# Reciprocals of softmax row sums: from a VectorE instruction to a GpSimd power of -1

## The reference

```python
q = (x @ Wq) ...; k = (x @ Wk) ...; v = (x @ Wv) ...     # 16 query heads, 4 key/value heads, 64 wide, rotary
attn = einsum('bhqd,bhkd->bhqk', q, k) / sqrt(64) + slopes * rel
attn = softmax(attn, axis=-1)                            # rows of 256 keys, for 16 heads x 256 queries
x = layernorm(x + (attn @ v) @ Wo)
x = layernorm(x + windowed_cross_attention(x, context))
x = layernorm(x + quantised_gated_ffn(x))
```

## Time and profile before

| | |
|---|---|
| median of 3 runs | 2327.14 us |
| the profiled execution, its own time | 2328.01 us |
| its span, first to last instruction | 2326.2 us |
| instructions | 54958 |
| mean granted TensorE clock | 0.985 |
| TensorE busy (matmul) | 2229.3 us, 96% |
| VectorE busy | 1976.2 us, 85% |
| ScalarE busy | 1568.7 us, 67% |
| GpSimd busy | 1220.2 us, 52% |

### The profile page before, as it was taken

One profiled execution on the slowest core, in us unless ns is written; L12 is line 12 of the kernel. 1 busy time (PEld: TensorE's weight loads), 2 busy tenths in 40 slices (PEclk: granted clock), 3 DMA queues, 4 the chain that ended last, 5 costly groups with the idle time before them and its releaser, 6 DMA issues.

```text
span 2326.2 us, 54958 instructions
## 1 busy us (share of the span) xinstructions
PE 2229.3 (96%) x18218; PEld 1644.8 (71%) x18218; DVE 1976.2 (85%) x8167; ACT 1568.7 (67%) x4449; POOL 1220.2 (52%) x1390
## 2 busy tenths in 40 slices
PE   5899999999999999999999999999999999999974
PEld 4666677777777777777777777777777777777752
DVE  5778888888888888888888888888888888888865
ACT  2477666777766777767677766677776667776741
POOL 2445555555555555565555555555556555555531
PEclk8899999999999999999999999999999999999997
DMA  5000110110011111011011001111101111100100
GB/s 169 27 11 24 28 36 26 35 36 23 23 36 35 27 36 30 18 34 36 27 35 35 22 24 35 34 28 35 31 15 35 35 27 35 36 22 23 36 10 14
DMA packets 84662, 74.69 MB, mean 32 GB/s; under 512 B 18336, under 2 KB 79136, under 8 KB 84384
## 3 DMA queue, kind: packets, MB, share of 16 engines
q1 hardware_dynamic: 84384, 71.19, 11.3%
HBM read 45.98 MB, written 8.39 MB: 23 GB/s over the span
## 4 chain that ended last, share of the span: by engine, by line
PE 83%; DVE 9%; ACT 3%; POOL 2%; issue 2%; SPq 1%; DMA 1%; DVEq 0%; POOLq 0%; ACTq 0%
PE bank L444 20%; PE bank L456 11%; PE bank L539 9%; PE bank L558 9%; PE bank L462 9%; PE bank L569 8%; PE bank L610 3%; PE bank L636 3%; PE bank L617 3%; PE bank L688 2%; PE bank L449 2%; PE bank L665 2%; PE bank L675 2%; POOL qx_tok L1200 2%; DVE q_sin L858 1%
## 5 line engine op out<-in xcount | busy, mean ns | idle before, releaser
L1177 POOL TENSOR_TENSOR prob<-prob,precs 128x512 f32<-128x512 f32 x512 | 542.9, 1076 | 381.9 <-DVE precs L821 381.8
L1092 ACT ACTIVATE prob<-prob,nmax 128x256 f32<-128x256 f32 x1024 | 508.2, 498 | 260.1 <-DVE nmax L814 260.1
L814 DVE CUSTOM_DVE_ANT_0 prob<-bank,alibi 128x256 f32<-128x256 f32 x1024 | 372.8, 420 | 63.7 <-PE bank L539 58.9
L1099 ACT COPY pT<-bank 128x512 f32<-128x512 f32 x512 | 298.7, 583 | 143.9 <-PE bank L444 143.9
L1116 ACT ACTIVATE px<-px,nmx 128x128 f32<-128x128 f32 x1024 | 314.0, 392 | 70.0 <-DVE nmx L919 70.0
L444 PE MATMUL bank<-ident,prob 128*128 128x128 f32 x2048 | 316.6, 277 | 10.1 <-ACT pT L1099 8.4
L444 PEld LDWEIGHTS bank<-ident,prob 128*128 128x128 f32 x2048 | 237.7, 141 | 79.1 <-issue 43.7
L539 PE MATMUL bank<-kk,qq 64*128 64x256 f32 x2048 | 291.9, 404 | 0.7 <-DVE nmax L814 0.7
L919 DVE CUSTOM_DVE_ANT_0 px<-bank,mask 128x128 f32<-128x128 f32 x1024 | 225.7, 284 | 44.2 <-PE bank L617 32.6
L558 PE MATMUL bank<-pT,v_sb 128*64 128x256 f32 x2048 | 249.3, 385 | 0.0
L539 PEld LDWEIGHTS bank<-kk,qq 64*128 64x128 f32 x2048 | 177.5, 187 | 55.1 <-issue 34.7
(11 more groups left out here) (194 smaller groups left out, 5004.1 us busy)
## 6 DMA issues: line engine op xcount, KB each, us to landing
xT<-in_xT SPq DMA_DIRECT2D x32, 256.0 KB, 4.1
kx_tok<-in_ctx SPq DMA_DIRECT2D x32, 256.0 KB, 3.7
cT<-in_ctxT SPq DMA_DIRECT2D x32, 256.0 KB, 2.8
xtok<-in_x SPq DMA_DIRECT2D x32, 256.0 KB, 3.0
kx<-k_sin SPq DMA_DIRECT2D x256, 32.0 KB, 2.0
vs<-vx SPq DMA_DIRECT2D x64, 128.0 KB, 2.5
out_y<-y SPq DMA_DIRECT2D x32, 256.0 KB, 2.2
cellk<-in_cell SPq DMA_DIRECT2D x32, 64.0 KB, 3.7
```

The source lines that it names most:

```text
L814: v.tensor_tensor_reduce(out=prob[:, (2 * p + q) % SLOTS, c, :], in0=psum[SCORES[c]][:, q * L:(q + 1) * L], in1=alibi[:, p % 2, c, :], sca ...
L1092: nc.scalar.activation(prob[:, (2 * p + q) % SLOTS, c, :], prob[:, (2 * p + q) % SLOTS, c, :], ACT.Exp, bias=nmax[:, i:i + 1], scale=-1.0, ...
L1099: nc.scalar.copy(pT[:, p % 2, :, :, q * P:(q + 1) * P].rearrange("p c k n -> p (c k) n"), bank[:].rearrange("p (c n) -> p c n", c=4)).then ...
L1177: g.tensor_tensor(prob[:, n % SLOTS, :, :], prob[:, n % SLOTS, :, :], precs[:, 2 * n:2 * n + 2].unsqueeze(2).to_broadcast([P, 2, L]), ALU. ...
```

## The change

VectorE's part of `R n` goes. GpSimd's part now waits for the exponentials itself, adds one to a spare semaphore, makes `precs` with a tensor_tensor of `psums` and a 128x2 tile of -1.0 under the operation `pow`, and waits for the end of that before it multiplies. The tile of -1.0 is set once at the start, which is one more memset on GpSimd. Nothing is moved in the three lists.

```diff
+        minus_one = sb("minus_one", [P, 2])
...
-        POOL_CONSTS = 8
+        POOL_CONSTS = 9
...
@@ VectorE
-                    elif kind == "R":
-                        n, = args
-                        dve.wait_ge(*at("p_exp", b, 2 * n + 1))
-                        v.reciprocal(precs[:, 2 * n:2 * n + 2], psums[:, 2 * n:2 * n + 2]).then_inc(sem["p_recip"], 1)
@@ GpSimd
                     elif kind == "R":
                         n, = args
+                        pool.wait_ge(*at("p_exp", b, 2 * n + 1))
+                        pool.sem_inc(waits_passed, 1)
+                        g.tensor_tensor(precs[:, 2 * n:2 * n + 2], psums[:, 2 * n:2 * n + 2], minus_one[:], ALU.pow).then_inc(sem["p_recip"], 1)
                         pool.wait_ge(*at("p_recip", b, n))
                         g.tensor_tensor(prob[:, n % SLOTS, :, :], prob[:, n % SLOTS, :, :],
                                         precs[:, 2 * n:2 * n + 2].unsqueeze(2).to_broadcast([P, 2, L]), ALU.mult)\
                             .then_inc(sem["p_norm"], 1)
...
+            g.memset(minus_one[:], -1.0).then_inc(pool_consts, 1)
             g.memset(ones[:], 1.0).then_inc(pool_consts, 1)
-            pool.wait_ge(pool_consts, 5)
+            pool.wait_ge(pool_consts, 6)
```

## The result

The changed kernel takes 2340.40 us (median of 4, 2338.92 to 2341.13) against 2327.05 us of the kernel before (median of 4, 2326.09 to 2327.27): the ratio is 1.0057, with a 95% interval of 1.0040 to 1.0075. It is **slower by some 13 us**, where 2.6 were forecast, and 1.4 us outside the range. The profiled execution took 2338.92 us, 10.91 more than the one of before (2328.01).

What follows compares the result with a forecast made beforehand. TensorE was taken as the bound, with rounds adding 0. First and last batches summed to +2.6 us, giving 2330.6 against the profiled 2328.01, or 2329.7 us for the median; range 2325 to 2339.

Steps and rivals of the forecast that it cites:

- T 9: In each BODY round, behind R 9 after `X1`: its margin falls from 1.1 to 0.3 us, the tightest of 16.
- A: Slower: R 9 behind `X1` grows by over 1.1 us, T 9 waits in every round; 2342 us, chance 0.1.
- B: Slower: at each round's second HC, R 14's multiply starts before waiting VectorE; +27 us, 2354 us, chance 0.06.
- C: Faster: VectorE's relief removes TensorE's waits at XQ and NO, half those in first batches; -9 us, 2318 us, chance 0.06.
- R starts when the exponentials are there: In every R step: gives back up to 8 us of queueing wherever GpSimd was idle.
- a: First batches, `qtok` at 73.40: R 10 behind the next `qtok` ends 0.8 us later, delaying T 10; +0.8 us.
- b: First batches, three R steps at 181.45 push `y_rstd` to 188.9, needed by VectorE at 188.07; +0.9 us.
- c: First batches, two longer R steps ahead of `YS` delay the norm; the shift of QN comes late; +0.4 us.
- d: First batches, four R steps at 278.44: the second ends 1.6 us later, T 7 starts at 281.32; +0.8 us.
- f: Last batches, two R steps at 2188.53 end at 2192.2, `QX` had started at 2191.06, TensorE waiting; +1.1 us.
- Term e: Last batches, two R steps kept QN's shift until 2178.64; it now starts when VectorE's scale is ready; -0.7 us.
- GpSimd against VectorE: Port conflict at a BODY round's HC steps: a power holds VectorE's second HC 0.3 us, covered by idle time; 0.

Runs made afterwards that it cites:

- the repeat: The changed kernel itself measured once more, on the chip of three later runs, against the kernel before: 2339.06 us, ratio 1.0052.
- the run with the cheap operation: Changed kernel with the power replaced by a multiplication by the same -1 tile on GpSimd, same waits: 2325.98 us against 2327.00, ratio 0.9998.

## Why the prediction was wrong

**The bound and the rounds: right.** The work of a round did not get longer: the lag stays at 9.3 to 10.4 us over all 27, and the three waits of the stage are equal to 0.1 us. T 9 kept 0.3 us of margin, as forecast, although the first power behind X1 was itself held by VectorE's rounding of the first HC:

```profile
1051.98 1.16 POOL L1175 TENSOR_TENSOR precs<-psums,minus_one 128x2 f32<-128x2 f32 x1
1053.22 1.04 POOL L1177 TENSOR_TENSOR prob<-prob,precs 128x512 f32<-128x512 f32 x1
...
1054.58 0.59 PEld L445 LDWEIGHTS bank<-ident,prob 128*128 128x128 f32 x4
```

The first multiply ends at 1054.26. Rivals A and B did not happen, nor C: without its reciprocals in the rounds VectorE bought nothing (ratio 0.9992). What was only half seen is why the rounds hold. "R starts when the exponentials are there" was entered as a help wherever GpSimd was idle, and the cost as hidden in idle time; the run with both a power and a reciprocal shows that without this help each round would cost 0.68 us at XQ and NO. Both places were named in the rivals, but neither rival had this cause.

**The price: right.** 697 ns in the median (758 in the mean, with the powers that were held) and 78 ns of gap, against 720 and 80.

**The terms a to f: mostly right.** Found (forecast): a 0.6 to 1.1 (0.8), b 0.7 to 0.9 (0.9), c 0.8 (0.4), d 0.4 to 0.7 (0.8), f 1.0 (1.1). Term e (-0.7) is not to be found in the changed kernel's trace. Nor does any run show the 0.7 us counted for VectorE's relief in the first and last batches: the one stretch in which TensorE caught up is there without that relief too. Not counted were 0.9 us at V, where GpSimd's multiply of R 2 ran beside products of VectorE, and 0.6 at 227. With four steps back on VectorE the measured loss is 4.0 us by the medians and 4.9 by the ratio (1.0021 of 2327), nearer to the forecast's 2.6 and within its own range of 2325 to 2335.

**The step that failed** is the part "GpSimd against VectorE". It went through the port's conflict in a round of BODY only, at the two HC steps, and the list for the first batches went by queueing alone. But the first batches hold VectorE's one-time steps (the split of Wo, prep 7, prep 8), with operations of 128x2048 that take 1.2 to 2.3 us each, two or three in a row. This term was put at nothing. Two T steps became late by 2.7 and 2.0 us (3.3 less 0.65, and 4.6 less 2.6, in the lag), and the work behind both, at the low clock, cost 1.8 and 2.1: 8.6 us (7.8 in the repeat). One step back on VectorE gives 5.05 us; VectorE waiting for that same step gives 3.64 us with all powers in place; four steps back give 8. For the first of the two places the cause is shown by experiment. At the second the hold is seen in the traces, and its price is not parted from that of three longer steps.

The working was wrong in a second place, with no price here. It let a power that runs across the start of the second HC hold VectorE for 0.3 us. The opposite is seen, in all 27 rounds:

```profile
1070.75 0.99 POOL L1175 TENSOR_TENSOR precs<-psums,minus_one 128x2 f32<-128x2 f32 x1 [0.74 <-ACT prob L1089]
...
1071.02 0.68 DVE L1014 TENSOR_SCALAR hq<-hh 128x1024 bf16<-128x1024 f32 x1
```

The power began 0.27 us before the rounding, and the rounding took its plain 0.68 us; it was the power that took 0.29 us more.

**The Trainium skill**, "SBUF — State Buffer", section "SBUF: two separate sides", says that a GpSimd operation and a VectorE operation in a two-port mode or with two SBUF inputs exclude each other: whichever starts first has the shared pair for the whole instruction, and the other fully blocks. For the multiply the runs agree: begun 0.25 us ahead of the cast, it kept its 1.04 us, and the cast took 1.87 and not 1.22. For the power they don't: begun 0.53 us ahead of the cast, it ended at 58.13, with the cast, whose 1.22 us were untouched. Here the measurement decides: a power in progress can't be counted on to keep the pair.

**The range** had its upper end at 2339, from half of a rival in the rounds. A bound for R steps that meet VectorE's long operations was missing from the sum, though such a row stood in it, 1.55 us for a step of 0.68.

## What to carry to other kernels

An operation that is moved to a queue is to be held against every long SBUF operation of the other engine that it can now meet, in the one-time steps at the start as much as in the rounds. Half a microsecond more on GpSimd cost 3.6 to 5 us at one place, since it decided which of two engines went first. And a lag between two single traces is not all the change's: from 85 to 121 us it moved by 2.8 us in a run whose steps there were those of before. A product that is freed from another engine's queue starts earlier as well as taking longer: both have to be followed, since here the one paid for the other in each round.

## What the runs showed of the hardware

- A GpSimd power of 128x2 takes 697 ns in the median, a multiplication of the same shapes 197 ns (`precs` of the changed kernel, and of the run with the cheap operation).
- A power of GpSimd that is under way as VectorE begins a long cast, scaling or rounding ends only after it (1.79, 1.70 and 0.99 us, in place of 0.70; the last in 27 of 27 rounds, 0.04 us behind the rounding); a GpSimd multiply of 128x512 that is under way holds the cast instead (1.87 us for 1.22 with the cheap operation, 1.84 in the run with a power and a reciprocal).
- VectorE's subtraction of 128x2048 with both inputs in SBUF (2.29 us) held a multiply that began 0.08 us behind it, which took 3.11 us: longer than the subtraction, by 0.9 of its own 1.04.
